# A fused attention and expert layer on one core: the router as four f32r passes with stationary weights, expert weights turned on VectorE, and a new order of VectorE's work

## The chip, the core and the metric

The kernel runs on 1 core of one Trainium2 chip. The metric is device time in microseconds (us). The engines are TensorE (PE, its weight loads PEld), VectorE (DVE), ScalarE (ACT), GpSimd (POOL) and SyncE (SP, which issues most transfers here). A single measurement of this kernel differs from another by some 0.1%; 0.2% is taken as what can be told from no change.

## The reference, cut to what matters

```python
x = L0_attn_x                                    # 8 x 2048 x 256, float32
x = x + attention(layernorm(x))                  # linear attention: Q (K^T V) sqrt(3/D) Wo, D = 64
h = layernorm(x)                                 # rows of 256
scores = sigmoid(h @ Wr)                         # Wr: 256 x 8, the router
_, idx = top_k(scores + router_bias, 2)
w = take(scores, idx); w = w / (sum(w) + 1e-9)
cw = zeros(T, 8).at[idx].add(w)                  # combining weights of 8 experts
hid = silu(h @ Wg[e]) * (h @ Wu[e])              # e = 0..3, inner width 128
routed = sum_e cw[:, e] * (hid @ Wd[e])
routed += cw[:, 4] * h + cw[:, 6] * h + cw[:, 7] * relu(h)
shared = causal_conv(h, conv_w, 4 taps) + conv_b # per channel, over a sequence of 2048
out = x + routed + shared
```

## The kernel before

The 16384 tokens are worked in 32 groups of 512 tokens (4 tiles of 128). The work on a group is cut into stages, and the stages of different groups run beside each other: in one step of the kernel a group is normalised (stage `L`), another's Gram matrix is summed (`A`), a third gets its queries (`Q`), a fourth its attention and second norm (`B`), a fifth is transposed and routed (`R`), a sixth goes through experts and convolution (`C`), a seventh is written out (`Y`). `LAG` says how many steps a stage lies behind stage `L`. Each engine runs a list of instructions that is written out by hand in its `body(st)`, step by step; nothing is scheduled by a planner, and engines wait for each other by semaphores (`wait_ge`). A head of its own starts the pipeline; `body` covers steps 7 to 39. In steps 9, 13, ..., 33 a new sequence begins, and a chain of small products (`chain_gramT`, `chain_p1`, `chain_et`, `chain_f`) makes its attention matrix: a chain step. The other 20 of the steps 7 to 33 are called normal here. Steps 34 to 37 have no `A`, `L` and `Q` work left and run in another order (`drain`).

Float32 products that carry most of the work are done as three f32r products of a high and a low part (`three`, lines 410 to 412): ACT rounds the high part, DVE subtracts it to get the low part (`hid_low`, `x2T_low`, `xn_low`).

What the change touches, in one normal step:

- PE: `gate_up(st, 0..7)` are gate and up products of the four experts, `down` the way back. `x2_transpose` turns the normalised group, ACT copies it out twice (`x2T_out`: full and high part), DVE makes the low part (`x2T_low`). `router` (lines 535 to 544) multiplies the plain float32 transposed tokens, 128 tokens stationary, by the 8 router columns. `weights_transpose` (line 600) turns the combining weights so that a row is one expert's.
- ACT: `logits_copy`, `score_size`, `score_dip` begin the sigmoid; `weights_copy` takes the turned weights out of PSUM; `norm2` (line 842) writes the next group to be transposed.
- DVE: `conv_tap(st, n)` are three of the four convolution taps, two instructions each (line 1073); `norm1_stats` and `norm2_stats` are row statistics; `route_scores` and `route_weights` finish the routing; `hidden` multiplies up by gate, `residual` adds the attention.
- POOL: `gate_weight(st, e)` multiplies the gate by the broadcast weights (line 1391), `norm_factors` makes scale and shift of a norm, `last_low` is the low part of the fourth expert (line 1396), `skip_factors` and `relu_add` belong to the skip experts.
- SP: `spread_weights` stores the turned weights to HBM and loads each of 4 rows back to all partitions (`cwb`).

## Time and profile before

| | us |
|---|---|
| median of 3 runs (885.03 to 885.51) | 885.39 |
| the profiled execution | 888.19 |
| its span, first to last instruction | 886.4 |

| engine | busy us | share of the span | instructions |
|---|---|---|---|
| PE | 852.9 | 96% | 5437 |
| PEld | 757.1 | 85% | 5437 |
| DVE | 751.2 | 85% | 2093 |
| ACT | 643.2 | 73% | 1366 |
| POOL | 409.6 | 46% | 585 |

Busy PE time is modelled from starts, since matmuls overlap in the array: what a matmul costs is better read from the distance to the next one's start. The mean granted clock of TensorE is 0.988 of full speed. Times inside the kernel are counted in the profiled execution; its span is what stages add up to, and the 1.8 us around it come on top.

### The profile page before, as it was taken

The numbers are of one execution on the slowest core, as the hardware profiler recorded it, in microseconds if no ns is written. First come the engines' busy times: TensorE is split into PE (matmuls) and PEld (weight loads), VectorE is DVE, ScalarE is ACT, GpSimd is POOL, SyncE is SP. The second block draws the span as 40 slices with busy tenths as digits, with TensorE's granted clock in tenths as the row PEclk, the third lists the DMA queues.
The fourth block names the chain that finished last, engine by engine and source line by source line (L and its number), as shares of the span: only waits on it lengthen the run. The fifth ranks groups of instructions, "written<-read, shape, count | busy, mean of one in ns | idle before, by whom it ended". The sixth has DMA issues, their size and how long they took to land.

```text
span 886.4 us, 16852 instructions
## 1 busy us (share of the span) xinstructions
PE 852.9 (96%) x5437; PEld 757.1 (85%) x5437; DVE 751.2 (85%) x2093; ACT 643.2 (73%) x1366; POOL 409.6 (46%) x585
## 2 busy tenths in 40 slices
PE   5878999999999999999999999999999999899997
PEld 4667888999889988889899998889988998788886
DVE  4668889988899988999899998999889988678884
ACT  4585867787777777787678777777867875666653
POOL 3214635554455454455355544545535544433332
PEclk9899999999999999999999999999999999999999
DMA  9112354433354442434443344554424344324434
GB/s 286 60 43 54 119 144 138 112 110 100 116 143 143 143 120 67 126 125 138 143 121 104 100 132 120 143 144 126 111 75 131 109 121 119 96 54 118 118 94 119
DMA packets 79447, 103.86 MB, mean 117 GB/s; under 512 B 6528, under 2 KB 58880, under 8 KB 79360
## 3 DMA queue, kind: packets, MB, share of 16 engines
q1 hardware_dynamic: 74752, 86.02, 30.6%
q0 software_dynamic: 4608, 16.78, 10.0%
q8 instruction: 43, 0.70, 0.3%
q14 instruction: 44, 0.36, 0.1%
HBM read 68.96 MB, written 17.04 MB: 97 GB/s over the span
## 4 chain that ended last, share of the span: by engine, by line
PE 77%; DVE 12%; ACT 4%; issue 3%; POOL 2%; DMA 1%; POOLq 0%; DVEq 0%; ACTq 0%
PE ps_gu L410 11%; PE ps_gu L412 10%; PE ps_gu L411 10%; PE ps_sh L541 6%; PE ps_y L410 6%; PE ps_y L411 6%; PE ps_y L412 6%; PE ps_y L460 3%; PE ps_sh L531 3%; PE ps_sh L484 2%; ACT x L842 2%; PE ps_sh L588 1%; PE ps_sh L589 1%; PE ps_gram L618 1%; PE ps_gu L564 1%
## 5 line engine op out<-in xcount | busy, mean ns | idle before, releaser
L1391 POOL TENSOR_TENSOR gate<-gate,cwb 128x512 f32<-128x512 f32 x128 | 168.0, 1313 | 291.4 <-ACT gate L765 265.6
L410 PE MATMUL ps_gu<-x2T_hi,wgu_hi 128*128 128x512 f32 x512 | 211.3, 413 | 1.2 <-DVE hid L1055 1.2
L412 PE MATMUL ps_gu<-x2T_hi,wgu_lo 128*128 128x512 f32 x512 | 202.2, 395 | 0.0
L411 PE MATMUL ps_gu<-x2T_lo,wgu_hi 128*128 128x512 f32 x512 | 201.7, 394 | 0.0
L410 PE MATMUL ps_y<-wd_hi,hid_hi 128*128 128x256 f32 x512 | 153.1, 299 | 2.2 <-DVE hid_lo L1062 2.2
L1073 DVE SCALAR_TENSOR_TENSOR conv<-x2T,conv_w,conv 128x512 f32<-128x512 f32 x192 | 150.6, 822 | 0.0
L411 PE MATMUL ps_y<-wd_lo,hid_hi 128*128 128x256 f32 x512 | 145.4, 284 | 0.0
L412 PE MATMUL ps_y<-wd_hi,hid_lo 128*128 128x256 f32 x512 | 145.0, 283 | 0.0
L1062 DVE TENSOR_TENSOR hid_lo<-hid,hid_hi 128x512 fp32r<-128x512 f32 x101 | 86.2, 853 | 46.2 <-ACT hid_hi L758 46.2
L412 PEld LDWEIGHTS ps_gu<-x2T_hi,wgu_lo 128*128 128x128 f32 x512 | 96.6, 189 | 22.2
L410 PEld LDWEIGHTS ps_gu<-x2T_hi,wgu_hi 128*128 128x128 f32 x512 | 97.2, 190 | 18.4 <-issue 2.3
L411 PEld LDWEIGHTS ps_gu<-x2T_lo,wgu_hi 128*128 128x128 f32 x512 | 97.4, 190 | 13.4
L1055 DVE TENSOR_TENSOR hid<-ps_gu,gate 128x512 f32<-128x512 f32 x128 | 86.2, 673 | 20.8 <-issue 13.3
L410 PEld LDWEIGHTS ps_y<-wd_hi,hid_hi 128*128 128x128 f32 x512 | 97.9, 191 | 4.9 <-DVE hid_lo L1062 3.5
L765 ACT ACTIVATE gate<-ps_gu 128x512 f32<-128x512 f32 x128 | 75.5, 590 | 33.5 <-PE ps_gu L412 32.7
L411 PEld LDWEIGHTS ps_y<-wd_lo,hid_hi 128*128 128x128 f32 x512 | 98.0, 191 | 1.6
L412 PEld LDWEIGHTS ps_y<-wd_hi,hid_lo 128*128 128x128 f32 x512 | 97.5, 190 | 0.0
L758 ACT ACTIVATE hid_hi<-hid 128x512 fp32r<-128x512 f32 x128 | 80.2, 626 | 18.5 <-DVE hid L1055 17.6
L1370 POOL TENSOR_TENSOR mv<-mv,eps_ln 128x4 f32<-128x4 f32 x64 | 24.3, 380 | 136.9 <-DVE mv L1112 114.0
L826 ACT ACTIVATE xn<-xa,shift,rstd 128x256 f32<-128x256 f32 x128 | 66.0, 591 | 6.5 <-POOL shift L1375 6.4
L1373 POOL TENSOR_TENSOR rstd<-mv,half_neg 128x4 f32<-128x4 f32 x64 | 67.4, 1054 | 5.0
L842 ACT ACTIVATE x<-acc,shift,rstd 128x256 f32<-128x256 f32 x128 | 66.3, 593 | 4.3 <-POOL shift L1375 4.2
(126 smaller groups left out, 1877.5 us busy)
## 6 DMA issues: line engine op xcount, KB each, us to landing
cwb<-cw_rows SPq DMA_DIRECT2D x128, 256.0 KB, 4.0
xa<-in_x SPq DMA_DIRECT2D x32, 512.0 KB, 7.8
acc<-in_x SPq DMA_DIRECT2D x32, 512.0 KB, 6.9
acc<-x POOLq DMA_DIRECT2D x32, 512.0 KB, 4.6
out<-acc SPq DMA_DIRECT2D x64, 256.0 KB, 2.6
cwb<-in_wg SPq DMA_DIRECT2D x4, 128.0 KB, 3.9
cwb<-in_wu SPq DMA_DIRECT2D x4, 128.0 KB, 3.7
cwb<-in_wd SPq DMA_DIRECT2D x1, 512.0 KB, 4.5
```

The costliest lines, as they stand in the source:

```text
L410: nc.tensor.matmul(dst, a_hi, b_hi, start=start, stop=False, skip_group_check=True)
L411: nc.tensor.matmul(dst, a_hi, b_lo, start=False, stop=False, skip_group_check=True)
L412: return nc.tensor.matmul(dst, a_lo, b_hi, start=False, stop=stop, skip_group_check=True)
L758: return nc.scalar.activation(dst, src, ACT.Copy, scale=scale)
L765: nc.scalar.activation(gate[:, e % 2], ps_gu[GU_BANK[2 * e]][:, :], ACT.Silu)\
L826: nc.scalar.activation(xn[:, q, t], xa[:, q, t], ACT.Identity, bias=shift1[:, f, t:t + 1], scale=rstd1[:, f, t:t + 1]).then_inc(xn_ready, 1)
L842: nc.scalar.activation(x2[:, q, t], acc[:, st.slot("B", 4), t], ACT.Identity, bias=shift2[:, q, t:t + 1], scale=rstd2[:, q, t:t + 1]).then ...
L1055: v.tensor_tensor(hid[:, e % 2], ps_gu[GU_BANK[2 * e + 1]][:, :], gate[:, e % 2], ALU.mult)\
L1062: v.tensor_tensor(hid_lo[:, k], hid[:, k], hid_hi[:, k].bitcast(F32), ALU.subtract)\
L1073: v.scalar_tensor_tensor(conv[:, c], x2T[:, q, c, k:k + GT], conv_w[:, c, k:k + 1], conv[:, c], ALU.mult, ALU.add).then_inc(conv_ready, 1)
L1373: g.tensor_tensor(rstd, mv[:, :, 1], half_neg[:, :], ALU.pow).then_inc(rstd_ready, 1)
L1391: g.tensor_tensor(gate[:, e % 2], gate[:, e % 2], cwb[:, q, e], ALU.mult).then_inc(gatew_ready, 1)
```

## The change

The router runs after the two low parts exist, with the weights stationary: `wr2` holds the 8 columns of `Wr` as high part and 8 as low part, so that 2 passes over the high part of the tokens and 2 over the low part (c = 0, 1) give all of it in 16 rows of PSUM, 512 tokens wide. ACT copies them (`logitsT_copy`), four transposes turn them (`logits_rows`), DVE adds the two halves (`logits_sum`). The combining weights are turned on DVE in blocks of 32 by 32, straight after `cw`, and stored by four transfers in place of one. On DVE the second pair of taps comes directly behind the first, `x2T_low(st, 1)` behind `output(st, 0)` and `hidden(st, 0)`, the statistics of norm 1 behind the second `hidden`, and `hid_low(st, 2)` between the two halves of the routing. On ACT the size of the scores is taken after the copy of the second expert's high part, and `hid_high(st, 2)` and `silu(st, 3)` go ahead of `conv_begin`. On POOL `skip_factors` moves into the next step, and `relu_add` ahead of the fourth `gate_weight`.

```diff
+        wr2 = sb("wr2", [P, HC, 2 * NE], F32R)
+        logitsT = sb("logitsT", [2 * NE, GT])
+        cwT = sb("cwT", [P, SQ])
...
@@ sync: spread_weights
-                sp.dma_start(rows.rearrange("a e (t n) -> (a e t) n", t=TG), cwT[:, :]).then_inc(cw_stored, 16)
-                sp.wait_ge(cw_stored, st.before("R", 16, 16))
+                for j in range(P // SQ):
+                    sp.dma_start(rows[:, :, :].rearrange("a e (t n) -> (a e t) n", t=TG)[:, j * SQ:(j + 1) * SQ],
+                                 cwT[j * SQ:j * SQ + EM * TG, :]).then_inc(cw_stored, 16)
+                sp.wait_ge(cw_stored, st.before("R", 64, 64))
@@ tensor
             def router(st):
-                pe.wait_ge(x2T_ready, st.before("R", HC, HC))
+                if st.before("R") == 0:
+                    pe.wait_ge(wrlo_out, 1)
+                b, q = ps_sh[0][0:2 * NE, :], st.slot("R", 2)
                 pe.wait_ge(x2Tlo_ready, st.before("R", HC, 1))
-                b, q = ps_sh[0], st.slot("R", 2)
+                pe.wait_ge(x2Thi_ready, st.before("R", HC, HC))
+                for c in range(HC):
+                    nc.tensor.matmul(b, wr2[:, c], x2T_hi[:, q, c], start=(c == 0), stop=False,
+                                     skip_group_check=True)
+                for c in range(HC):
+                    if c == 1:
+                        pe.wait_ge(x2Tlo_ready, st.before("R", HC, HC))
+                    last = nc.tensor.matmul(b, wr2[:, c], x2T_lo[:, q, c], start=False, stop=(c == HC - 1),
+                                            skip_group_check=True)
+                last.then_inc(router_done, 1)
+
+            def logits_rows(st):
+                pe.wait_ge(logitsT_ready, st.before("R", 1, 1))
                 for t in range(TG):
-                    for c in range(HC):
-                        last = nc.tensor.matmul(b[:, t * NE:(t + 1) * NE],
-                                                x2T[:, q, c, PAD + t * P:PAD + (t + 1) * P], wr_sb[:, c],
-                                                start=(c == 0), stop=(c == HC - 1))
-                last.then_inc(router_done, 1)
+                    last = nc.tensor.transpose(ps_sh[0][:, t * 2 * NE:(t + 1) * 2 * NE],
+                                               logitsT[0:2 * NE, t * P:(t + 1) * P], ident[0:2 * NE, 0:2 * NE])
+                last.then_inc(rows_done, 1)
...
@@ tensor: body
                 if c_on:
                     gate_up(st, 3)
+                if r_on:
+                    logits_rows(st)
...
-                if r_on:
-                    weights_transpose(st)
                 if a_on and r_on:
                     xn_transpose(st, 0)
@@ scalar
-                copy(logits[:, :], ps_sh[0][:, 0:TG * NE]).then_inc(logits_ready, 1)
-                nc.scalar.activation(size[:, :], ps_sh[0][:, 0:TG * NE], ACT.Abs).then_inc(logits_ready, 1)
+                copy(logitsT[:, :], ps_sh[0][0:2 * NE, :]).then_inc(logitsT_ready, 1)
...
-            def weights_copy(st):
@@ scalar: body
                 if r_on:
-                    logits_copy(st)
+                    logitsT_copy(st)
                 if m_on:
                     f_copy(st)
-                if r_on:
-                    score_size(st)
                 if c_on:
                     hid_high(st, 0)
-                if r_on:
-                    score_dip(st)
...
+                if r_on:
+                    score_size(st)
+                    score_dip(st)
...
-                if c_on and st.drain():
+                if c_on:
                     hid_high(st, 2)
                     silu(st, 3)
                 if r_on:
                     conv_begin(st)
-                if c_on and not st.drain():
-                    silu(st, 3)
-                    hid_high(st, 2)
                 if st.on("L"):
                     norm1(st)
-                if r_on:
-                    weights_copy(st)
@@ vector
+                dve.wait_ge(cw_ready, st.before("R", 1, 1))
+                if st.later("R", 1):
+                    dve.wait_ge(cw_stored, st.before("R", 64))
+                v.transpose(cwT[:, :], cw[:, q].rearrange("p e t -> p (e t)")).then_inc(cwT_ready, 1)
+
+            def logits_sum(st):
+                dve.wait_ge(rows_done, st.before("R", 1, 1))
+                v.tensor_reduce(logits[:, :].rearrange("p (t e) -> p t e", t=TG),
+                                ps_sh[0][:, 0:TG * 2 * NE].rearrange("p (t h e) -> p t e h", t=TG, h=2), AXX, ALU.add)\
+                    .then_inc(logits_ready, 1)
@@ vector: body
                     conv_tap(st, 0)
-                if st.on("L"):
-                    norm1_stats(st)
+                    conv_tap(st, 1)
                 if r_on and st.later("C", 1):
                     x2T_low(st, 0)
-                if c_on:
-                    conv_tap(st, 1)
+                if y_on:
+                    output(st, 0)
+                if c_on and st.later("C", 1):
+                    hidden(st, 0)
                 if r_on and st.later("C", 1):
                     x2T_low(st, 1)
                 if y_on:
-                    output(st, 0)
                     output(st, 1)
...
                     hidden(st, 1)
+                if r_on:
+                    logits_sum(st)
                 if m_on:
                     f_low(st)
...
+                if st.on("L"):
+                    norm1_stats(st)
                 if c_on:
                     hid_low(st, 1)
+                if st.on("L"):
+                    norm1_aggr(st)
...
                 if r_on:
                     route_scores(st)
-                if c_on and drain:
+                if c_on:
                     hid_low(st, 2)
                 if r_on:
                     route_weights(st)
-                if c_on and not drain:
-                    hid_low(st, 2)
@@ gpsimd: body
                     gate_weight(st, 0)
+                    skip_factors(st)
                     gate_weight(st, 1)
...
                     norm1_factors(st)
-                    if st.drain():
-                        relu_add(st)
+                    relu_add(st)
...
                     gate_weight(st, 3)
-                if c_on and not st.drain():
-                    relu_add(st)
...
-                if r_on:
-                    skip_factors(st)
```
```

The order of PE before, in a normal step, around the router (`ps_gu<-x2T_hi,wgu` are gate and up products of the third and fourth slot, L541 the router):

```order
L412 MATMUL ps_gu<-x2T_hi,wgu_lo 128x512
L541 MATMUL ps_sh<-wr_sb,x2T 128x8 x8
L410 MATMUL ps_gu<-x2T_hi,wgu_hi 128x512
L411 MATMUL ps_gu<-x2T_lo,wgu_hi 128x512
L412 MATMUL ps_gu<-x2T_hi,wgu_lo 128x512
L410 MATMUL ps_gu<-x2T_hi,wgu_hi 128x512
L411 MATMUL ps_gu<-x2T_lo,wgu_hi 128x512
L412 MATMUL ps_gu<-x2T_hi,wgu_lo 128x512
```

The same place in the changed kernel (L547 and L552 are the router's passes over high and low part, L559 the four transposes of the logits):

```order
L421 MATMUL ps_gu<-x2T_hi,wgu_lo 128x512
L547 MATMUL ps_sh<-x2T_hi,wr 16x512 x2
L552 MATMUL ps_sh<-x2T_lo,wr 16x512 x2
L419 MATMUL ps_gu<-x2T_hi,wgu_hi 128x512
L420 MATMUL ps_gu<-x2T_lo,wgu_hi 128x512
L421 MATMUL ps_gu<-x2T_hi,wgu_lo 128x512
L419 MATMUL ps_gu<-x2T_hi,wgu_hi 128x512
L420 MATMUL ps_gu<-x2T_lo,wgu_hi 128x512
L421 MATMUL ps_gu<-x2T_hi,wgu_lo 128x512
L559 MATMUL ps_sh<-ident,logitsT 128x16 x4
L419 MATMUL ps_gu<-x2T_hi,wgu_hi 128x512
```

Eight float32 products of 8 columns have become four f32r products of 512 columns in the same place, and four transposes have come in behind the next gate-and-up product; the transpose of the weights (L600), which stood between the Gram products and the turned rows of the next group, is gone.

The order of DVE before, from the last low parts of one normal step into the next (L1073 taps, L1186 low part of the turned tokens, L1224 output, L1055 hidden product, L1090 and L1093 statistics of norm 1, L1062 low part of hidden):

```order
L1235 TENSOR_TENSOR xnT<-ps_sh,xnT 128x512 x2
L1073 SCALAR_TENSOR_TENSOR conv<-x2T,conv_w,conv 128x512 x2
L1090 BN_STATS stats<-xa 128x6 x4
L1046 COPY tick<-ident 1x1
L1093 BN_AGGR mv<-stats 128x2 x4
L1186 TENSOR_TENSOR x2T_lo<-ps_sh,x2T_hi 128x512
L1073 SCALAR_TENSOR_TENSOR conv<-x2T,conv_w,conv 128x512 x2
L1186 TENSOR_TENSOR x2T_lo<-ps_sh,x2T_hi 128x512
L1224 TENSOR_TENSOR acc<-ps_y,acc 128x512 x2
L1055 TENSOR_TENSOR hid<-ps_gu,gate 128x512
L1073 SCALAR_TENSOR_TENSOR conv<-x2T,conv_w,conv 128x512 x2
L1062 TENSOR_TENSOR hid_lo<-hid,hid_hi 128x512
```

The same place in the changed kernel (L1063 taps, L1192 low part, L1233 output, L1043 hidden product, L1185 the sum of the logits, L1080 statistics, L1052 low part of hidden):

```order
L1244 TENSOR_TENSOR xnT<-ps_sh,xnT 128x512 x2
L1063 SCALAR_TENSOR_TENSOR conv<-x2T,conv_w,conv 128x512 x4
L1192 TENSOR_TENSOR x2T_lo<-ps_sh,x2T_hi 128x512
L1233 TENSOR_TENSOR acc<-ps_y,acc 128x512
L1043 TENSOR_TENSOR hid<-ps_gu,gate 128x512
L1192 TENSOR_TENSOR x2T_lo<-ps_sh,x2T_hi 128x512
L1233 TENSOR_TENSOR acc<-ps_y,acc 128x512
L1063 SCALAR_TENSOR_TENSOR conv<-x2T,conv_w,conv 128x512 x2
L1052 TENSOR_TENSOR hid_lo<-hid,hid_hi 128x512
L1043 TENSOR_TENSOR hid<-ps_gu,gate 128x512
L1185 TENSOR_REDUCE logits<-ps_sh 128x32
L1080 BN_STATS stats<-xa 128x6 x4
```

Both pairs of taps now run one behind the other, the two low parts of the turned tokens stand apart, and the statistics come after the second hidden product and the sum of the logits.

The order of DVE before, in the routing (L1157 copies the best two, L1165 and L1167 pick the weights, L1179 scales them, L1101 is the residual):

```order
L1157 COPY two<-top 128x4x2
L1046 COPY tick<-ident 1x1
L1165 MATCH_REPLACE marked<-two,biased 128x14 x4
L1167 SCALAR_TENSOR_TENSOR raw<-marked,score 128x4x8
L1170 TENSOR_REDUCE wsum<-raw 128x4
L1172 RECIPROCAL winv<-wsum 128x4
L1179 TENSOR_TENSOR cw<-raw,winv 128x4x8
L1062 TENSOR_TENSOR hid_lo<-hid,hid_hi 128x512
L1101 TENSOR_TENSOR acc<-ps_sh,acc 128x512 x2
```

The same place in the changed kernel (L1154, L1162, L1164, L1175 and L1098 for these; L1181 turns the weights):

```order
L1154 COPY two<-top 128x4x2
L1052 TENSOR_TENSOR hid_lo<-hid,hid_hi 128x512
L1034 COPY tick<-ident 1x1
L1162 MATCH_REPLACE marked<-two,biased 128x14 x4
L1164 SCALAR_TENSOR_TENSOR raw<-marked,score 128x4x8
L1167 TENSOR_REDUCE wsum<-raw 128x4
L1169 RECIPROCAL winv<-wsum 128x4
L1175 TENSOR_TENSOR cw<-raw,winv 128x4x8
L1181 STREAM_TRANSPOSE cwT<-cw 128x32
L1098 TENSOR_TENSOR acc<-ps_sh,acc 128x512 x2
```

The low part of the third expert's hidden product (L1062, now L1052) has moved from behind the weights into the middle of the routing, and the turn of the weights has come in ahead of the residual.

## Rows read from the trace of the kernel before

**Rows 1.** Busy time by engine in four steps (us, instructions, clock, DMA).
```profile
204.09:308.18 104.09, 103.96 (x681) 93.14 (x680) 93.78 (x262) 80.37 (x172) 53.27 (x72) 1.00 0.42 123
```

**Rows 2.** Timeline of PE, one normal step: start us, us, what.
```profile
197.26 0.60 PE L531 MATMUL ps_sh<-ident,x 128*128 128x128 f32 x4
197.61 0.36 PE L410 MATMUL ps_y<-wd_hi,hid_hi 128*128 128x256 f32 x1
...
200.96 1.84 PE L541 MATMUL ps_sh<-wr_sb,x2T 128*128 128x8 f32 x16
202.66 0.48 PE L410 MATMUL ps_gu<-x2T_hi,wgu_hi 128*128 128x512 f32 x1
202.98 0.39 PE L411 MATMUL ps_gu<-x2T_lo,wgu_hi 128*128 128x512 f32 x1
...
203.21 0.39 PE L412 MATMUL ps_gu<-x2T_hi,wgu_lo 128*128 128x512 f32 x1
...
222.38 0.60 PE L531 MATMUL ps_sh<-ident,x 128*128 128x128 f32 x4
```

**Rows 3.** Timeline of DVE, the same step.
```profile
197.46 1.40 DVE L1090 BATCH_NORM_STATS2 stats<-xa 128x6 f32<-128x256 f32 x4
...
201.74 1.27 DVE L1224 TENSOR_TENSOR acc<-ps_y,acc 128x512 f32<-128x512 f32 x2
202.94 0.67 DVE L1055 TENSOR_TENSOR hid<-ps_gu,gate 128x512 f32<-128x512 f32 x1
...
209.93 0.69 DVE L1055 TENSOR_TENSOR hid<-ps_gu,gate 128x512 f32<-128x512 f32 x1 [0.51 <-issue]
...
212.35 0.17 DVE L1157 COPY two<-top 128x8 f32<-128x8 f32 x1
...
215.01 1.28 DVE L1101 TENSOR_TENSOR acc<-ps_sh,acc 128x512 f32<-128x512 f32 x2
...
217.83 0.36 DVE L1112 BATCH_NORM_AGGREGATE mv<-stats 128x2 f32<-128x6 f32 x4
```

**Rows 4.** Timeline of POOL and ACT, the same step and the next one's start.
```profile
212.48 1.30 POOL L1391 TENSOR_TENSOR gate<-gate,cwb 128x512 f32<-128x512 f32 x1 [1.63 <-ACT gate L765]
...
219.91 0.20 POOL L1375 TENSOR_TENSOR shift<-negm,rstd 128x4 f32<-128x4 f32 x1
220.14 1.30 POOL L1396 TENSOR_TENSOR hid_lo<-hid,hid_hi 128x512 fp32r<-128x512 f32 x1
...
220.44 2.07 ACT L842 ACTIVATE x<-acc,shift,rstd 128x256 f32<-128x256 f32 x4
```

**Rows 5.** Timeline of DVE and POOL, the start of step 7.
```profile
71.95 2.69 DVE L1073 SCALAR_TENSOR_TENSOR conv<-x2T,conv_w,conv 128x512 f32<-128x512 f32 x4
...
72.56 3.81 POOL L1391 TENSOR_TENSOR gate<-gate,cwb 128x512 f32<-128x512 f32 x1 [3.53 <-ACT gate L765]
```

**Rows 6.** Timeline of DVE and POOL, a chain step.
```profile
221.19 1.46 DVE L1073 SCALAR_TENSOR_TENSOR conv<-x2T,conv_w,conv 128x512 f32<-128x512 f32 x2
...
228.91 2.44 DVE L1073 SCALAR_TENSOR_TENSOR conv<-x2T,conv_w,conv 128x512 f32<-128x512 f32 x2
233.92 0.69 DVE L1062 TENSOR_TENSOR hid_lo<-hid,hid_hi 128x512 fp32r<-128x512 f32 x1 [2.58 <-ACT hid_hi L758]
...
235.99 1.43 DVE L1062 TENSOR_TENSOR hid_lo<-hid,hid_hi 128x512 fp32r<-128x512 f32 x1 [0.32 <-ACT hid_hi L758]
...
221.39 0.66 POOL L1423 TENSOR_TENSOR coef<-cw 128x4 f32<-128x4 f32 x1
...
228.87 1.26 POOL L1391 TENSOR_TENSOR gate<-gate,cwb 128x512 f32<-128x512 f32 x1 [3.96 <-ACT gate L765]
```

**Rows 7.** Who waited for whom, PE: total us, times, longest.
```profile
PE ps_y L460 <- DVE conv L1073: 2.9, 1, 2.9
...
PE ps_sh L600 <- DVE cw L1179: 1.0, 4, 0.4
```

**Rows 8.** Timeline of SP's queue, the last group's weights.
```profile
861.25 0.33 SPq L353 DMA_DIRECT2D cw_rows<-cwT  x1
```

More of the change, by code:

```diff
@@ L508, in xn_transpose @@
                 pe.wait_ge(xn_ready, st.before("A", TG, TG))
-                if c == 1 and st.on("R"):
-                    pe.wait_ge(cwT_ready, st.before("R", 1, 1))
-                elif st.on("B"):
+                if st.on("B"):
                     pe.wait_ge(x1_ready, st.before("B", 2, 2 - c))
@@ L579, in attention @@
                 elif st.before("B") > 1:
[L580 removed]
+                    pe.wait_ge(logits_ready, st.before("R", 1, 1))
                 if h == 0:
@@ L740, in body @@
                     gram_halves(st)
-                if drain:
-                    down(st, "C", 2)
-                if r_on:
-                    weights_transpose(st)
                 if a_on and r_on:
                     xn_transpose(st, 0)
-                if c_on and not drain:
+                if c_on:
                     down(st, "C", 2)
@@ L888, in score_size @@
             def score_size(st):
-                act.wait_ge(logits_ready, st.before("R", 2, 2))
+                act.wait_ge(logits_ready, st.before("R", 1, 1))
                 if st.later("R", 1):
                     act.wait_ge(cw_ready, st.before("R"))
+                nc.scalar.activation(size[:, :], logits[:, :], ACT.Abs).then_inc(size_ready, 1)
+                act.wait_ge(size_ready, st.before("R", 1, 1))
                 nc.scalar.activation(mag[:, :], size[:, :], ACT.Identity, bias=least[:, :]).then_inc(mag_ready, 1)
@@ L909, in conv_begin @@
                         .then_inc(tap_ready, 1)
-            def weights_copy(st):
-                act.wait_ge(cwT_done, st.before("R", 1, 1))
-                if st.later("R", 1):
-                    act.wait_ge(cw_stored, st.before("R", 16))
-                copy(cwT[:, :], ps_sh[1][0:EM * TG, 0:P]).then_inc(cwT_ready, 1)
             def xnT_head(n, c):
@@ L960, in head @@
                 conv_begin(r)
-                weights_copy(r)
                 q_high(at("Q", 4, NG))
@@ L1060, in hid_low @@
                 dve.wait_ge(hidhi_ready, st.before("C", EM, e + 1))
+                if e == 1 and st.on("L"):
+                    dve.wait_ge(stat1, st.before("L", TG, TG))
                 k = e % 2
@@ L1090, in norm1_stats, with norm1_aggr, norm1_both @@
                     v.bn_stats(stats1[:, f, t], xa[:, q, t]).then_inc(stat1, 1)
-                turn(stat1, st.before("L", TG, TG))
+            def norm1_aggr(st):
+                f = st.slot("L", 2)
                 for t in range(TG):
                     v.bn_aggr(mv1[:, f, t], stats1[:, f, t]).then_inc(aggr1, 1)
+            def norm1_both(st):
+                norm1_stats(st)
+                turn(stat1, st.before("L", TG, TG))
+                norm1_aggr(st)
             def residual(st, h):
@@ L1299, in body @@
                 if y_on:
-                    output(st, 0)
                     output(st, 1)
                 if c_on:
-                    if st.later("C", 1):
-                        hidden(st, 0)
                     conv_tap(st, 2)
@@ L1327, in body @@
                     route_weights(st)
-                if c_on and not drain:
-                    hid_low(st, 2)
                 if b_on and not drain:
```

73 lines of the change are left out of this document (35 added, 38 removed).

## The prediction

> **What bounds the kernel now.** I read the busy time of four steps first: PE is busy 103.96 of 104.09 us, DVE 93.78, ACT 80.37 [rows 1]. PE sets the pace; the step is as long as the sum of what PE issues. The timeline of PE shows the pieces by the distance between starts: from one turn of the tokens to the next a normal step takes 222.38 - 197.26 = 25.12 us [rows 2]; four steps with one chain step take 104.09, so a chain step takes 104.09 - 3 x 25.12 = 28.73. DVE's busy share is over nine tenths, so the second question is how far DVE can follow a shorter PE step. The third view is the timeline of the engines around the second norm, since one loop runs through all of them: statistics on DVE, factors on POOL, the norm on ACT, the turn on PE, and from there the products whose results DVE needs for its next statistics. The end of norm 2's aggregation (217.83 + 0.36 = 218.19, [rows 3]) is called E below. The reader is to see how little room lies between this loop and PE's own step.
>
> **PE, part by part, per normal step.** The old router takes 202.66 - 200.96 = 1.70, and the f32r product after it starts its successor 0.32 later instead of 0.23, so leaving float32 costs 0.09 [rows 2]: 1.79 goes. The new router is four passes of 512 columns at 0.23 (202.98 to 203.21): 0.92. No row has a stationary side of 16 columns; the bounds are 0.23 a pass, and nothing gained, 0.42 a pass, if it cost as much as the float32 product does for its share (1.70 / 4). I take 0.23, the nearest row in type and width. The four transposes of the logits resemble the four of the tokens, 197.61 - 197.26 = 0.35; they are narrower, so 0.35 is the upper end and 0.1 the lower; I take 0.35, and 0.09 for leaving float32 again. The turn of the weights, one transpose of the same kind, 0.09 to 0.11, goes, beside float32 transposes that stay. Sum: -1.79 - 0.11 + 0.92 + 0.44 = -0.54. If PE alone counted, a normal step would take 24.58, and a chain step would gain the same (there the change of type is paid once with `chain_f`).
>
> **The loop through DVE.** From E: POOL's shift is done at 219.91 + 0.20 = 220.11, 1.92 later [rows 4]; ACT's norm needs 0.04 and 2.07 (220.44); the last turned tile 0.18. So PE may go on to `down` at E + 4.21 at the earliest. From there (197.61) to DVE's third `hidden` (209.93) the trace has 12.32 [rows 2, 3]; this stretch holds the router and the logits' transposes, -1.79 + 0.92 + 0.44 = -0.43, so 11.89. From the third `hidden` to the residual (215.01) it has 5.08, and from there to E 3.18 [rows 3]. In the kernel before this makes 4.21 + 12.32 + 5.08 + 3.18 = 24.79, 0.33 below PE's step: hidden. Now three things are added:
>
> - The turn of the weights on DVE stands ahead of the residual. No row shows such an operation; 0.17 (a small copy, 212.35) and 0.69 (a full one, 209.93) bound it [rows 3]. I take 0.22, nearest to the small copy: 32 columns only.
> - `hid_low(st, 2)` runs inside the routing and POOL's fourth gate (1.30, 212.48) beside it. When a GpSimd product and a DVE product of two SBUF operands meet, one waits: in a chain step the gate started at 228.87, the taps at 228.91 took 2.44 instead of 1.39, and 1.05 was lost [rows 6]. In the step before, the fourth gate starts 212.48 - 209.93 = 2.55 after the third `hidden`, and both starts come from PE's products, whose distance stays. The copy of the best two starts 2.42 after, and its successor 0.08 later, at 2.50: `hid_low(st, 2)` is ahead by 0.05, the gate waits for it, and then delays the pick of the weights a little. I add 0.13, an estimate; 0 and 0.6 bound it.
> - The taps start later on DVE. `last_low` starts at E + 1.95 (220.14) and lets the taps go about 1.13 later, at E + 3.1. Four taps at 2.69 / 4 = 0.67 [rows 5] end at 5.8. The first gate, asked for meanwhile, waits until then and ends at 7.0. `x2T_low(st, 0)` and `output(st, 0)` (0.60 each, from 201.74 to 202.94) end at 7.0, `hidden(st, 0)` at 7.65, `x2T_low(st, 1)` at 8.25, seen by PE at about 8.35. The router's fourth pass would start at 4.21 + (200.96 - 197.61) + 3 x 0.23 = 8.25: it waits 0.1.
>
> New loop: 4.21 + 11.89 + 0.10 + 5.08 + 0.22 + 0.13 + 3.18 = 24.81, longer than PE's 24.58. So the loop sets the normal step, and it gains 25.12 - 24.81 = 0.31.
>
> **What is hidden, and its cover.** The sum of the logits on DVE (0.17 to 0.69, I take 0.25) and the statistics of norm 1 (1.43, from 197.46) now stand ahead of `hid_low(st, 1)`. There DVE waited 0.51 ahead of the third `hidden`; by the same walk DVE is ready for it some 0.2 before PE. If that cover is gone, each 0.1 more is 0.1 a step. The copy of the logits on ACT (16 rows of 512, as long as other copies of 512, about 0.6) is covered by the gate-and-up product between router and transposes, 6 x 0.23 = 1.39. `weights_copy` leaves ACT. Three more transfers for the weights lie well ahead of their use.
>
> **Chain steps.** There DVE waits 2.58 for ACT's copies of the chain and runs on almost without a wait to E [rows 6]. The router's gain reaches it (0.54), and the 0.32 wait and the stretch of 1.43 for a product of 0.67 go; but statistics (1.43), sum and turn (0.47) now come behind the wait. 0.54 + 0.32 + 0.76 - 1.43 - 0.47 = -0.28. With the norm's small slack I take 0 for a chain step, -0.6 to +0.5.
>
> **Ends.** Four drain steps are PE's: 0.54 and the wait for the weights, 1.0 / 4 = 0.25 [rows 7], 0.79 x 4 = 3.2. At step 7 PE waits 2.9 for the taps, once [rows 7]; statistics of 1.43 leave the way ahead of them, and with the router that is about 1.9. At the end three more issues of 0.33 [rows 8] stand ahead of the last loads of weights, against the way over PE and ACT, which I put at 0.5: a loss of 0.5.
>
> **Sum.** 20 x 0.31 + 0 + 3.2 + 1.9 - 0.5 = 10.8. The profiled execution's span of 886.4 becomes 875.6. The median, 885.39, lies 1.0 below that span; I subtract from it: 874.6, said as 874.5.
>
> **Rivals.**
> *PE keeps the pace.* DVE's loop is shorter than I walked it (turn and sum cheaper, a gate elsewhere). Then 27 steps gain 0.54: 14.6 + 4.6 = 19.2, 866. For it: PE's share of 103.96 in 104.09 [rows 1]. Against it: 24.79 for the loop before anything is added.
> *The fourth gate comes first.* A lead of 0.05 can turn. Then `hid_low(st, 2)` waits over 1 us, about 0.5 more a step than above: 25.3, 0.2 over before, 885.4 + 4 - 4.6 = 885. For it: 0.04 of lead decided between gate and taps [rows 6].
> *The first gate gets in between the taps*, the slower side. Then two taps wait about 1.1, `x2T_low(st, 1)` comes at 9.4, the router's fourth pass waits 1.2, the loop is 25.9 and the time 885.4 + 20 x 0.8 - 4.6 = 897. It turns the sign once the loss is over 0.5 a step. For it: POOL's small `coef`, asked for at 221.39, was done at 222.05, inside a pair of taps that ended at 222.65 [rows 6]. Against it: in step 7 a gate asked for at 72.56 took 3.81 instead of 1.30, while four taps took 2.69, undisturbed [rows 5]. The Trainium skill, SBUF — State Buffer, section SBUF: two separate sides, says that VectorE and GpSimd share a port pair, that whichever starts first holds it for its whole instruction, and that the other blocks. Read so, the pair is free between two taps, and this rival's 897 would be the time; the row of step 7 shows the waiting gate not getting it, which gives 874.5. I go by that row, as it has the same instructions.
> *The change doesn't pay.* PE's four passes cost 0.42: the normal step is 25.5 and the time some 890.
>
> **Chances.** My forecast 0.42, PE keeps the pace 0.24, the fourth gate first 0.15, taps split 0.11, dear passes 0.03, others 0.05. My case's own range is 870 to 879. For 8 in 10 I take in PE's pace and most of the fourth gate: 864 to 886. By the same cases: faster than before by over 0.2% (below 883.6) 0.71, within 0.2% (what a measurement can tell) 0.13, slower 0.16.
>
> **What would show it.** Right: normal steps of 24.6 to 24.9 from turn to turn; four router passes 0.23 apart; the first gate of a step stretched beyond 2 us while four taps take 2.7; the fourth gate starting behind `hid_low(st, 2)`. Wrong: taps of over 3 us with a gate inside; PE waiting for `x2T_lo` at the router for over 0.3; PE's waits for ACT's norm over 0.3 a step, which would mean a longer loop; chain steps above 29.

## The result and the profile after

The changed kernel takes 912.35 us (median of 4 runs, 910.37 to 915.34) against 885.21 us before: ratio 1.031, interval 1.028 to 1.035, slower. The forecast was 874.5 us. The profiled execution takes 910.77 us, with a span of 909.0 (before: 886.4).

I read the four steps from turn to turn first, as in [rows 1]: busy time of PE, PEld, DVE, ACT and POOL, then the granted clock.

```profile
224.44:330.99 106.55, 102.59 (x645) 87.61 (x644) 97.13 (x266) 82.53 (x168) 51.49 (x72) 1.00 0.40 118
```

Four steps take 106.55 us instead of 104.09. PE, which was busy to within 0.13 us, now idles 4 us of them, at full clock. So PE got less work, as forecast, and began to wait. The chain of waits on PE says for what (us in total, times, longest):

```profile
PE ps_sh L552 <- DVE x2T_lo L1192: 16.2, 21, 0.9
...
PE ps_sh L493 <- DVE acc L1098: 8.4, 6, 1.6
PE ps_sh L536 <- ACT x L846: 4.5, 7, 3.5
PE ps_y L419 <- DVE hid_lo L1052: 4.4, 5, 1.0
```

The first line is the router's fourth pass (L552), which waits for `x2T_low(st, 1)` in 21 steps; the second is the turn of `xn`, which waits for the residual in 6 of the 7 chain steps. Neither is among the waits of PE in the kernel before. The timeline of DVE in a normal step shows why the low part is late; E is 301.21 + 0.35 = 301.56:

```profile
301.21 0.35 DVE L1109 BATCH_NORM_AGGREGATE mv<-stats 128x2 f32<-128x6 f32 x4
...
304.15 4.14 DVE L1063 SCALAR_TENSOR_TENSOR conv<-x2T,conv_w,conv 128x512 f32<-128x512 f32 x4
308.22 0.68 DVE L1192 TENSOR_TENSOR x2T_lo<-ps_sh,x2T_hi 128x512 fp32r<-128x512 f32 x1
308.82 0.68 DVE L1233 TENSOR_TENSOR acc<-ps_y,acc 128x512 f32<-128x512 f32 x1
309.42 0.68 DVE L1043 TENSOR_TENSOR hid<-ps_gu,gate 128x512 f32<-128x512 f32 x1
310.02 0.68 DVE L1192 TENSOR_TENSOR x2T_lo<-ps_sh,x2T_hi 128x512 fp32r<-128x512 f32 x1
```

and POOL beside it:

```profile
303.43 1.29 POOL L1407 TENSOR_TENSOR hid_lo<-hid,hid_hi 128x512 fp32r<-128x512 f32 x1
306.22 1.53 POOL L1402 TENSOR_TENSOR gate<-gate,cwb 128x512 f32<-128x512 f32 x1 [1.49 <-ACT gate L768]
```

Four taps take 4.14 us, not 2.69: the first waits some 0.4 for `last_low`, and the first gate, asked for at 306.22, ran inside the run and held the fourth tap up by 1.0. The low part ends at 310.70 = E + 9.14. PE's timeline of the same step:

```profile
305.48 0.60 PE L536 MATMUL ps_sh<-ident,x 128*128 128x128 f32 x4
...
309.20 0.62 PE L547 MATMUL ps_sh<-x2T_hi,wr 128*16 128x512 f32 x2
309.66 0.40 PE L552 MATMUL ps_sh<-x2T_lo,wr 128*16 128x512 f32 x1
310.75 0.40 PE L552 MATMUL ps_sh<-x2T_lo,wr 128*16 128x512 f32 x1 [0.69 <-DVE x2T_lo L1192]
```

Three passes follow each other at 0.23; the fourth starts 1.09 after the third, 0.86 late.

The same trace has one normal step in which the gate stayed out of the taps. From 174.22 to 198.89 it waited for its row of weights and came only when the last tap was nearly done; DVE, then POOL:

```profile
172.90 3.13 DVE L1063 SCALAR_TENSOR_TENSOR conv<-x2T,conv_w,conv 128x512 f32<-128x512 f32 x4
```

```profile
175.84 1.34 POOL L1402 TENSOR_TENSOR gate<-gate,cwb 128x512 f32<-128x512 f32 x1 [2.35 <-DMA cwb<-cw_rows]
```

The taps took 3.13, no pass waited, and this step took 24.67 us where the other normal steps take 25.55.

In a chain step another thing is seen, on DVE:

```profile
349.71 1.71 DVE L1154 COPY two<-top 128x8 f32<-128x8 f32 x1
351.33 0.68 DVE L1052 TENSOR_TENSOR hid_lo<-hid,hid_hi 128x512 fp32r<-128x512 f32 x1
```

on POOL:

```profile
349.77 1.60 POOL L1402 TENSOR_TENSOR gate<-gate,cwb 128x512 f32<-128x512 f32 x1
```

The copy of the best two, 0.17 us in a normal step [rows 3], lasts as long as the fourth gate beside it, and 1.36 us of PE's wait at L493 follow (at 355.11).

Where the 22.6 us of the span between the turns went, by the starts of the turns of the tokens: 6 chain steps +4.7, the 6 steps behind them +4.0, 12 normal steps +4.4, the last two drain steps (35 and 36) and what follows +8.8, of which +5.0 lie behind the last turn; the rest +0.7. The steps behind the chain steps have the same wait of the fourth pass as normal ones, 0.78 to 0.83 in its row.

### The profile page after: what moved, and what is told of

Its sections match the earlier page's. It is cut to its first block, busy times and chain, and to the rows that moved or that the text cites. A ratio compares the mean times of both kernels' runs of the same rounds, so it can differ in the third digit from the quotient of the medians.

```text
span 909.0 us, 16313 instructions
## 1 busy us (share of the span) xinstructions
PE 842.9 (93%) x5149; PEld 713.9 (79%) x5149; DVE 776.4 (85%) x2133; ACT 657.6 (72%) x1335; POOL 401.8 (44%) x585
## 4 chain that ended last, share of the span: by engine, by line
PE 56%; DVE 26%; issue 8%; ACT 5%; POOL 2%; DMA 1%; POOLq 0%; DVEq 0%; SPq 0%; ACTq 0%
PE ps_gu L419 8%; DVE conv L1063 8%; PE ps_gu L421 8%; PE ps_gu L420 7%; PE ps_y L421 4%; PE ps_y L419 4%; PE ps_y L420 4%; DVE hid L1043 3%; DVE x2T_lo L1192 3%; PE ps_y L469 3%; PE ps_sh L493 2%; DVE stats L1106 1%; PE ps_sh L552 1%; PE ps_sh L605 1%; PE ps_gram L623 1%
## 5 line engine op out<-in xcount | busy, mean ns | idle before, releaser
L1402 POOL TENSOR_TENSOR gate<-gate,cwb 128x512 f32<-128x512 f32 x128 | 186.2, 1455 | 254.8 <-ACT gate L768 222.3
L419 PE MATMUL ps_gu<-x2T_hi,wgu_hi 128*128 128x512 f32 x512 | 211.5, 413 | 2.2 <-DVE hid L1043 2.2
L421 PE MATMUL ps_gu<-x2T_hi,wgu_lo 128*128 128x512 f32 x512 | 203.1, 397 | 0.0
L420 PE MATMUL ps_gu<-x2T_lo,wgu_hi 128*128 128x512 f32 x512 | 202.5, 396 | 0.0
L1063 DVE SCALAR_TENSOR_TENSOR conv<-x2T,conv_w,conv 128x512 f32<-128x512 f32 x192 | 170.6, 941 | 0.0
L419 PE MATMUL ps_y<-wd_hi,hid_hi 128*128 128x256 f32 x512 | 151.7, 296 | 4.4 <-DVE hid_lo L1052 4.4
L421 PE MATMUL ps_y<-wd_hi,hid_lo 128*128 128x256 f32 x512 | 144.7, 283 | 0.0
L420 PE MATMUL ps_y<-wd_lo,hid_hi 128*128 128x256 f32 x512 | 144.5, 282 | 0.0
L1052 DVE TENSOR_TENSOR hid_lo<-hid,hid_hi 128x512 fp32r<-128x512 f32 x101 | 84.8, 840 | 51.5 <-ACT hid_hi L761 50.4
L1381 POOL TENSOR_TENSOR mv<-mv,eps_ln 128x4 f32<-128x4 f32 x64 | 35.3, 552 | 192.1 <-DVE mv L1109 138.0
L768 ACT ACTIVATE gate<-ps_gu 128x512 f32<-128x512 f32 x128 | 75.6, 590 | 59.9 <-PE ps_gu L421 58.5
L421 PEld LDWEIGHTS ps_gu<-x2T_hi,wgu_lo 128*128 128x128 f32 x512 | 97.3, 190 | 22.2
L419 PEld LDWEIGHTS ps_gu<-x2T_hi,wgu_hi 128*128 128x128 f32 x512 | 97.5, 190 | 21.3 <-DVE hid L1043 4.1
L420 PEld LDWEIGHTS ps_gu<-x2T_lo,wgu_hi 128*128 128x128 f32 x512 | 97.5, 191 | 14.3
L761 ACT ACTIVATE hid_hi<-hid 128x512 fp32r<-128x512 f32 x128 | 79.8, 623 | 33.1 <-DVE hid L1043 33.0
L419 PEld LDWEIGHTS ps_y<-wd_hi,hid_hi 128*128 128x128 f32 x512 | 97.8, 191 | 6.9 <-DVE hid_lo L1052 5.4
L1043 DVE TENSOR_TENSOR hid<-ps_gu,gate 128x512 f32<-128x512 f32 x128 | 86.4, 675 | 17.7 <-POOL gate L1402 7.2
L420 PEld LDWEIGHTS ps_y<-wd_lo,hid_hi 128*128 128x128 f32 x512 | 97.4, 190 | 1.8
L421 PEld LDWEIGHTS ps_y<-wd_hi,hid_lo 128*128 128x128 f32 x512 | 97.1, 190 | 0.0
L846 ACT ACTIVATE x<-acc,shift,rstd 128x256 f32<-128x256 f32 x128 | 66.5, 591 | 14.6 <-issue 8.5
```

The lines of the kernel that those rows point to most:

```text
L419: nc.tensor.matmul(dst, a_hi, b_hi, start=start, stop=False, skip_group_check=True)
L420: nc.tensor.matmul(dst, a_hi, b_lo, start=False, stop=False, skip_group_check=True)
L421: return nc.tensor.matmul(dst, a_lo, b_hi, start=False, stop=stop, skip_group_check=True)
L761: return nc.scalar.activation(dst, src, ACT.Copy, scale=scale)
L768: nc.scalar.activation(gate[:, e % 2], ps_gu[GU_BANK[2 * e]][:, :], ACT.Silu)\
L846: nc.scalar.activation(x2[:, q, t], acc[:, st.slot("B", 4), t], ACT.Identity, bias=shift2[:, q, t:t + 1], scale=rstd2[:, q, t:t + 1]).then ...
```

## The experiments

Times are medians, ratios are to the kernel before on the same chip. The kernel before itself spread from 883.9 to 891.3 us over these comparisons, more than the 0.1% given at the start; the intervals are the better guide. Steps are read from one turn of the tokens to the next, in the middle of the run; "behind chain" is the step after a chain step, "drain" are the steps 35 and 36; "x2T_lo" is when `x2T_low(st, 1)` ends, from E, in a normal step.

```
kernel                 time   ratio [interval]      normal behind chain  drain        x2T_lo
                                                           chain
before                 885.2                        25.12  25.47  28.40  22.4         8.66
after                  912.4  1.031 [1.028, 1.035]  25.55  26.14  29.16  24.3         9.14
e1 gate 1 waits        897.7  1.015 [1.012, 1.017]  24.92  25.51  29.16  23.7         8.48
e2 low between taps    885.9  1.001 [0.999, 1.003]  24.69  25.20  29.16  22.4 to 22.7 8.26
e3 old DVE order       896.0  1.013 [1.011, 1.015]  25.44  25.65  28.13  22.9 to 23.7 8.65
e4 order alone         906.6  1.024 [1.023, 1.026]  25.50  25.61  29.44  25.1         8.33
e5 chain stats early   875.2  0.985 [0.982, 0.988]  24.69  24.81  27.59  22.4 to 22.8 8.25
e6 small gate 1        887.6  1.001 [0.999, 1.002]  24.69  25.17  29.17  23.3         8.18
e7 start alone         899.6  1.013 [1.009, 1.016]  25.11  25.57  29.20  23.5 to 25.1 8.50
e8 last pass later     893.0  1.007 [1.005, 1.010]  24.60  25.08  29.15  24.3 to 25.7 9.14
e9 drain, first step   873.5  0.985 [0.983, 0.987]  24.71  24.85  27.60  22.9         8.25
e10 last pass too      876.9  0.989 [0.987, 0.990]  24.91  25.06  27.59  22.6 to 22.9 8.26
e11 gate 4 in chain    881.3  0.994 [0.992, 0.996]  24.69  25.21  28.30  22.7 to 23.1
e12 both gates wait    891.2  1.007 [1.004, 1.010]  24.91  25.50  28.30  23.5 to 23.7
```

**e1: the first gate waits for the taps.** This makes true what the forecast took for granted.

```diff
 pool.wait_ge(gate_ready, st.before("C", EM, e + 1))
+if e == 0 and st.later("C", 1):
+    pool.wait_ge(conv_ready, st.before("C", CT, 2 * HC))
```

> The changed kernel, with the first gate's multiply on POOL made to wait for the fourth tap. Theory A, the failed step is the gate that got in between the taps: taps in one run of 2.7 to 3.1 us (4.14 after the change), x2T_low(1) about 0.7 earlier, the router's fourth pass waits 0.1 or less (0.69 to 0.83), normal steps near 24.8 instead of 25.6, and 890 to 898 us, since chain steps and drains keep their own losses. Theory B, any order leaves x2T_low(1) too late for the new router: the wait stays over 0.5 and the time within 5 us of 912. Theory C, the statistics behind the chain's wait are the whole loss: no change in normal steps.

Measured: 897.7 us, 14.6 less. DVE's timeline, then PE's waits:

```profile
303.68 3.12 DVE L1063 SCALAR_TENSOR_TENSOR conv<-x2T,conv_w,conv 128x512 f32<-128x512 f32 x4
```

```profile
PE ps_sh L552 <- DVE x2T_lo L1192: 4.6, 8, 1.2
```

The taps take 3.12, a normal step 24.92; the list has a wait of the fourth pass in 8 steps instead of 21, three of them drain steps. It isn't gone in the others: `hidden(st, 0)` now waits 0.25 for the gate, the low part ends at 8.48, and the fourth pass starts 0.22 late, which is too short for the list. A normal step gains 0.63 by a wait added.

**e6: the first gate cut to 4 columns**, order as changed. The other 508 columns of the first expert stay unweighted.

```diff
-g.tensor_tensor(gate[:, e % 2], gate[:, e % 2], cwb[:, q, e], ALU.mult)
+w = 4 if e == 0 else GT
+g.tensor_tensor(gate[:, e % 2, 0:w], gate[:, e % 2, 0:w], cwb[:, q, e, 0:w], ALU.mult)
```

> The changed kernel with the first gate's multiply cut to 4 of 512 columns (it leaves out the weighting of the other 508 for the first expert); order and waits as changed. Theory A, the multiply itself holds the taps: the run of taps shrinks from 4.14 to 3.1 us, no wait of the fourth pass over 0.1, normal steps 24.7, 893 to 898 us as with the gate behind the taps. If the taps are late for the order alone: taps stay over 3.8 and the time within 3 us of 912.

Measured: 887.6 us, lower than expected: normal steps are 24.69 as expected, but the steps behind the chain and the ends gain too. The small gate is asked for at the same place, E + 4.65, and takes 0.44. On DVE:

```profile
191.74 0.36 DVE L1109 BATCH_NORM_AGGREGATE mv<-stats 128x2 f32<-128x6 f32 x4
...
194.66 3.13 DVE L1063 SCALAR_TENSOR_TENSOR conv<-x2T,conv_w,conv 128x512 f32<-128x512 f32 x4
197.74 0.69 DVE L1192 TENSOR_TENSOR x2T_lo<-ps_sh,x2T_hi 128x512 fp32r<-128x512 f32 x1
199.60 0.69 DVE L1192 TENSOR_TENSOR x2T_lo<-ps_sh,x2T_hi 128x512 fp32r<-128x512 f32 x1
```

The run of taps is 1.01 shorter, 4.14 to 3.13, and nothing else in the program changed: the width of POOL's product is the cause. Chain steps stay at 29.17, so theirs is another. The busy times of a normal step, in the order given with the four steps above, show who sets the pace once the gate is out:

```profile
275.23:299.89 24.66, 24.66 (x157) 21.36 (x156) 23.63 (x67) 20.20 (x41) 11.99 (x18) 1.00 0.47 131
```

PE is busy in all 24.66 us of it. A short wait can hide in that, but no two starts in this step lie further apart than those around a change of type (0.27 to 0.34): the step is PE's own again, and the loop through DVE isn't longer than that.

**e8: the fourth pass waits behind other work**, DVE and POOL as changed.

```diff
-router(st); gate_up(st, 3); logits_rows(st); gate_up(st, 4)
+router(st, split); gate_up(st, 3); router_last(st); gate_up(st, 4); logits_rows(st)
```

> The changed kernel, DVE, POOL and ACT untouched; on PE the router's fourth pass goes behind the gate-and-up product that followed it, and the four transposes of the logits one product further back, in normal steps. Theory A, the late x2T_low(1) costs only by the fourth pass that waits for it: taps stay at 4.1 us with the gate inside, the wait goes, normal steps 24.7 to 24.9 instead of 25.55, 893 to 900 us. If DVE as a whole is what is late (hidden(0) and all behind it): normal steps stay over 25.3.

Measured: 893.0 us. On PE:

```profile
277.20 0.60 PE L536 MATMUL ps_sh<-ident,x 128*128 128x128 f32 x4
...
281.38 0.39 PE L554 MATMUL ps_sh<-x2T_lo,wr 128*16 128x512 f32 x1
282.99 0.39 PE L561 MATMUL ps_sh<-x2T_lo,wr 128*16 128x512 f32 x1
...
301.80 0.60 PE L536 MATMUL ps_sh<-ident,x 128*128 128x128 f32 x4
```

The gate still sits in the taps and the low part still ends at E + 9.14, but a normal step takes 301.80 - 277.20 = 24.60 without a wait. So in normal steps the late low part cost by that one pass alone. The same split on top of e9 does the reverse (e10).

**e2 and e3: the start of before on DVE, with and without its early statistics.**

```diff
 conv_tap(st, 0)
-conv_tap(st, 1)
 x2T_low(st, 0)
-output(st, 0); hidden(st, 0); x2T_low(st, 1); output(st, 1)
+conv_tap(st, 1); x2T_low(st, 1); output(st, 0); output(st, 1); hidden(st, 0)
```

e3 also puts `norm1_both(st)` behind `conv_tap(st, 0)` and `hid_low(st, 2)` behind the weights.

> The changed kernel with the start of before on DVE (two taps, x2T_low(0), two taps, x2T_low(1), both outputs, hidden(0)), statistics still late. The gate, asked for 4.7 us after the end of norm 2's aggregation, finds DVE waiting for x2T_hi (ends at 5.6), so it isn't between taps. Theory A: x2T_low(1) ends at 8.3, no wait of the fourth pass, but DVE then idles 1.2 us ahead of x2T_low(0) and is itself late for the third hidden: normal steps 25.0 to 25.3, 898 to 906 us. Theory B: the fourth pass still waits over 0.5, 908 us or more.

> The changed kernel with the whole DVE order of before in the steps (statistics between the first taps and x2T_low(0), hid_low(2) behind the weights); router, turn of the weights, ACT and POOL as changed. Theory A, the order with its gate between the taps made the change slow: 866 to 885 us, normal steps 24.6 to 25.1. Theory B, the new router needs x2T_low(1) sooner than this order delivers it (by the walk at 9.0 us against 8.3 wanted): the fourth pass waits 0.5 or more, normal steps 25.2 to 25.5, 888 to 900 us. Theory C: the chain steps' wait of xn_transpose for the residual (1.35 to 1.56) goes.

Measured: e2 885.9, better than expected; e3 896.0, as theory B has it, with a smaller wait. e2's DVE and POOL:

```profile
192.48 0.36 DVE L1109 BATCH_NORM_AGGREGATE mv<-stats 128x2 f32<-128x6 f32 x4
...
195.43 1.78 DVE L1063 SCALAR_TENSOR_TENSOR conv<-x2T,conv_w,conv 128x512 f32<-128x512 f32 x2
198.51 0.69 DVE L1192 TENSOR_TENSOR x2T_lo<-ps_sh,x2T_hi 128x512 fp32r<-128x512 f32 x1 [1.30 <-ACT x2T_hi L761]
199.12 1.41 DVE L1063 SCALAR_TENSOR_TENSOR conv<-x2T,conv_w,conv 128x512 f32<-128x512 f32 x2
200.44 0.68 DVE L1192 TENSOR_TENSOR x2T_lo<-ps_sh,x2T_hi 128x512 fp32r<-128x512 f32 x1
```

```profile
197.49 1.29 POOL L1402 TENSOR_TENSOR gate<-gate,cwb 128x512 f32<-128x512 f32 x1 [1.49 <-ACT gate L768]
```

The gate falls into DVE's wait of 1.30 and disturbs nothing; the low part ends at 201.12 = E + 8.28. With the statistics in that gap (e3) it ends at E + 8.65: in the old order the new router waits too (6.6 us in 20 steps at L552), and e3 is slower than before. A part of e3's loss is `hid_low(st, 2)`: from third `hidden` to residual it has 5.57, e2 5.25; the two edits were not tried apart. Neither order that was given suits the new router; a third one does.

**e4 and e7: the order alone, with the old router.** e4 is the kernel before with DVE's new order; e7 puts `hid_low(st, 2)` back behind the weights; the lines below are the part of e4 that e7 takes back.

```diff
-if c_on and drain: hid_low(st, 2)
+if c_on: hid_low(st, 2)
 route_weights(st)
```

> The kernel before with the new DVE order alone (taps and first products ahead, statistics late, hid_low(2) ahead of the weights); old router, old turn of the weights. Theory A with the late x2T_low(1) costing through the router only: the old router waits for x2T_low(0) alone, so normal steps stay at 25.1, and chain steps lose up to 1.0 by the statistics behind the chain's wait: 885 to 895 us. Theory C, the order is the whole loss: 905 us or more.

> The kernel of e4_order_alone (906.6 us) with hid_low(2) back behind the weights, as in the kernel before: what is left of the change is the start (taps, first products) and the late statistics, with the old router. In e4 the fourth gate came ahead of hid_low(2), which took 1.43 and held up the weights: 0.74 more between third hidden and residual. If that is e4's loss: normal steps 25.1, chain steps 28.8 to 29.2, 887 to 893 us. If the start itself costs with the old router too: normal steps 25.4 or more and over 898 us.

Measured: e4 906.6, the number of theory C, though not by its way: the low part ends at 8.33, and in normal steps no gate is inside the taps. e7 899.6, outside the expected 887 to 893: normal steps of 25.11 and chain steps of 29.20 are as expected, but two drain steps lose 1.1 and 2.6, which I had not expected. e4's DVE and POOL show the difference:

```profile
211.70 1.43 DVE L1064 TENSOR_TENSOR hid_lo<-hid,hid_hi 128x512 fp32r<-128x512 f32 x1 [0.36 <-ACT hid_hi L758]
```

```profile
211.29 1.29 POOL L1400 TENSOR_TENSOR gate<-gate,cwb 128x512 f32<-128x512 f32 x1 [1.22 <-ACT gate L765]
```

ACT's order is the old one there (`silu(st, 3)` ahead of `hid_high(st, 2)`), so the fourth gate comes first: from third `hidden` to residual 5.82 us, against 5.07 in e7 (5.25 in e2, with the turn of the weights on the way). With the old router the new start costs nothing in normal steps (e7). So the order alone costs 2.4% with the old router too (e4), but in normal steps at another place: behind the third `hidden`, not at the taps.

**e5 and e11: the chain steps.** Both start from e2. e5 puts norm 1's statistics back behind the first taps in chain steps alone; e11 leaves them late and lets the fourth gate wait there.

```diff
 # e5
 conv_tap(st, 0)
+if st.on("L") and m_on: norm1_both(st)
 # e11
+if e == 3 and st.chain():
+    pool.wait_ge(hidlo_ready[0], st.before("C", EM // 2, 2))
```

> The kernel of e2_low_between_taps (882 to 890 us), with norm 1's statistics back in their old place in the chain steps alone, where DVE otherwise idles 1.7 us ahead of x2T_low(0). If the chain steps' loss is the statistics behind the chain's wait: xn_transpose's waits for the residual (8.4 us in 6) go, chain steps fall from 29.15 to about 28.05 us as in e3_old_order, normal steps stay at 24.7, 875 to 880 us and faster than the kernel before. If DVE is late there for another reason (the turn of the weights, hid_low(2)): chain steps stay over 28.8 and the time within 2 us of e2.

> The kernel of e2_low_between_taps (885.9 us; statistics late) with POOL's fourth gate made to wait for hid_low(2) in the chain steps alone. In e2 and after the change the copy of the best two (0.17 us elsewhere) takes 1.70 there, since the gate is asked for beside it. Theory D, it is again a multiply of POOL that came first, not the statistics themselves: the copy is back at 0.17, the residual comes 1.3 to 1.5 sooner, xn_transpose's waits (8.4 us in 6) go, chain steps 27.6 to 27.9 instead of 29.15, 876 to 879 us. Theory C, the statistics behind the chain's wait are the loss: chain steps stay over 28.7 and the time over 883.

Measured: e5 875.2, faster than both kernels. e11 881.3, between the two theories: chain steps 28.30, the copy back at 0.17, and of the residual's wait this is left:

```profile
PE ps_sh L493 <- DVE acc L1098: 3.2, 6, 0.7
```

So of the 1.57 that a chain step loses against e5, the fourth gate in the wrong place is 0.86 and the late statistics themselves 0.71; one brought the other about, since with early statistics the copy comes before the gate.

**e12: both gates wait**, order as changed (the edits of e1 and e11).

> The changed kernel, its order on every engine untouched, with two waits more on POOL: the first gate behind the fourth tap (as in e1_gate_behind_taps, 897.7 us), and in chain steps the fourth gate behind hid_low(2). If the two multiplies of POOL that came first are what made the change slow inside the loop: normal steps 24.9, chain steps 27.7 to 28.0, 887 to 891 us, what is left above e5 being drains and ends (5 to 8 us) and 0.2 a step. If one of them only hides a wait of the same length: 895 us or more.

Measured: 891.2, 0.2 above the expected range; normal steps 24.91 as expected, chain steps 28.30, over the expected 27.7 to 28.0, since the late statistics are still in them. Two waits on POOL give back 21.1 of the 27.1 us.

**e9 and e10: the ends, and the last pass once more.** e9 is e5 with `logits_sum(st)` ahead of `hid_low(st, 0)` in drain steps, and the first taps ahead of `hidden(st, 0)` in step 7; e10 adds the split of e8.

> The kernel of e5_chain_stats_early (875.2 us) with two moves on DVE at the ends: in the drain steps the sum of the logits goes ahead of hid_low(0), and in the first full step (step 7) the first taps go ahead of hidden(0), whose gate waits there for the loaded weights, with the statistics late again in that one step. If the drains' missing gain is the second attention's wait for the sum (0.7 a step, 3 shown): 22.4 becomes 21.7 to 21.9 a drain step, 2 to 2.8 us in all. If PE's wait of 3.3 us for the taps at step 7 is the late start of the taps: it shrinks below 1.5. Together 869 to 873 us. If the waits only move to the products behind them: 874 to 876.

> The kernel of e9 with the router's fourth pass behind the following gate-and-up product in normal steps, as in e8_last_pass_later. There a normal step took 24.60 against 24.69 in e5; PE changes matrix type one time less next to the router. If that difference is PE's own: normal steps 24.60, about 1.5 to 2 us below e9. If it is the loop through DVE: the same time as e9 within 1 us.

Measured: e9 873.5, the lowest time here, though its ratio is that of e5. At step 7 PE's wait for the taps fell from 3.3 to 0.7. In the drains the wait for the logits went, but the wait for `hid_lo` grew (e5: 1.9 us in 4, now 3.6 in 4) and a drain step takes 22.9, no less than in e5: there the wait only moved, as the last sentence of the expectation has it. e10 is 3.4 slower than e9, against expectation. Its PE:

```profile
303.11 0.40 PE L561 MATMUL ps_sh<-x2T_lo,wr 128*16 128x512 f32 x1
303.54 0.50 PE L419 MATMUL ps_gu<-x2T_hi,wgu_hi 128*128 128x512 f32 x1
```

There 0.43 lie between two starts that are 0.23 apart elsewhere. The product at 303.54 needs the bank that `hidden(st, 0)` empties, and in this order that ends at 303.48; the split brought the product forward into a wait. In e8 `hidden(st, 0)` is 1.5 earlier.

## Why the prediction was wrong

**The step that failed** is "The first gate, asked for meanwhile, waits until then and ends at 7.0". The gate got in at the end of the third tap. `x2T_low(st, 1)` ended at E + 9.14 instead of 8.25, and the fourth pass, forecast to wait 0.1, started 0.86 late. That is the rival on the slower side ("the first gate gets in between the taps"), with 9.4 and a loop of 25.9 forecast, 9.14 and 25.55 measured. I gave it 0.11. Taking this gate out of the taps is worth 14.6 of the 27.1 us (e1), and with the fourth gate of the chain steps 21.1 (e12). So it isn't the whole error: e1 is still slower than the kernel before, and chain steps and drains below have their own.

The Trainium skill, SBUF — State Buffer, section SBUF: two separate sides, says that whichever of the two engines starts first holds the shared pair for its whole instruction. The trace agrees: in the row at 306.22 the gate took 1.53, that is a remainder of a tap and its own 1.29. The same section of the Trainium skill names a DVE operation in a two-port mode as one that can be shut out. The copy of 1.71 at 349.71 fits that, though its row begins 0.06 before the gate's, and no run shows in which mode it ran.

I had set [rows 5] against that rule, one event. By my count over the 14 traces, a full-width gate asked for inside a run of such DVE products got in at the next end in 70 of 76 cases, 47 of them in the changed kernel and e8; the six others all lie between 72.0 and 75.7 us, in step 7. What is different there was not found. The row for it that I named, POOL's small `coef` done inside a pair of taps [rows 6], was the better witness: it too got in at the end of a tap.

**The rest of the walk held, but not what it was to show.** Take the gate away, and the places on the way are within 0.15 (forecast, e6): low part 8.25 and 8.18 from E, third `hidden` 16.20 and 16.27, residual 21.63 and 21.52. e2 gives the same by order alone. But "So the loop sets the normal step" did not come true: in e6 PE has no idle time left, so its 24.69 is PE's step, and the loop is no longer than that, against 24.81 forecast. Without the gate it is the rival "PE keeps the pace" that is seen. With the full gate where the forecast puts it, behind the taps, the step is 24.92 (e1), since `hidden(st, 0)` then waits for the gate.

**PE's terms were nearly right.** Four passes at 0.23, so the rival of dear passes is out; the next product 0.35 behind the first of the transposes; on DVE the turn of the weights 0.21 (0.22 forecast), the sum of the logits 0.21 (0.25):

```profile
L1181 DVE STREAM_TRANSPOSE cwT<-cw 128x32 f32<-128x32 f32 x32 | 6.8, 211 | 1.3 <-DVE cw L1175 0.2
L1185 DVE TENSOR_REDUCE logits<-ps_sh 128x32 f32<-128x64 f32 x32 | 6.7, 209 | 1.2 <-PE ps_sh L559 1.2
```

The columns before the last bar are busy us and mean ns. With nothing to wait for PE's step is 24.67 in the changed order (the step at 174.22, e6), against 24.58 forecast: the product ahead of the logits' transposes takes 0.32 (180.03 to 180.35) instead of 0.23, a price for the change from f32r into float32 that the sum had not. In e8, where one such change less stands beside the router, it is 24.60. **The fourth gate** stood where forecast in normal steps, behind `hid_low(st, 2)`; e4 against e7, with the old router, shows what that rival costs from third `hidden` to residual: 0.75, where about 0.5 was forecast.

**Chain steps** were put at 0 (-0.6 to +0.5) and lost 0.76. The sum left out that with DVE later (third `hidden` 1.0 later from E than in e5) the fourth gate comes first there: the rival that I had only looked for in normal steps. e11 prices it at 0.86; without it a chain step is at 28.30, 0.10 under the kernel before, so the rest of that sum came out. (28.73 was no chain step's time: the four steps hold one behind a chain step too, and the two take 28.40 and 25.47. The sum doesn't use it.)

**Drains and end** were put at -3.2 and +0.5 and lost 8.8 in the last two steps and the tail. There are no statistics there, but the taps start behind `hid_low(st, 3)`, and four taps with a gate inside now stand ahead of both low parts. With the gate cut to 4 columns a drain step takes 23.3 instead of 24.3 (e6). PE, drain step:

```profile
816.52 0.63 PE L547 MATMUL ps_sh<-x2T_hi,wr 128*16 128x512 f32 x2 [0.77 <-DVE x2T_lo L1192]
816.99 0.40 PE L552 MATMUL ps_sh<-x2T_lo,wr 128*16 128x512 f32 x1
818.31 0.41 PE L552 MATMUL ps_sh<-x2T_lo,wr 128*16 128x512 f32 x1 [0.93 <-DVE x2T_lo L1192]
```

1.70 of waits here, and 0.90 for `hid_lo`; before, a drain step waited 0.31 for `hid_lo` and 0.20 for the weights. From 864 to 870, where these waits stand once more and PE was busy for 4.3 of the 6 us, the mean granted clock was 0.79 (full 2.4 GHz, for a part 1.2). With the low parts between the taps the drain is back at 22.4 to 22.8 (e2, e5), but the forecast 21.6 was reached by none: a wait that goes is taken over by the next (e9). Which loop bounds the drain was not settled, nor how the 5.0 behind the last turn divide up.

**Step 7** was put at -1.9; PE's wait for the taps went from 2.9 to 2.6 only, since the taps stand behind a `hidden(st, 0)` whose gate waits for loaded weights. e9 removes that.

The price of three more stores, and the 0.5 set against it, were not tried apart.
